# Cross-attention and feed-forward block on one core: later contexts in another place, first weight unit in halves, zeros multiplied, other orders

## The reference

```python
query = einsum('bnc,dc->bnd', ctx, Wq) + bq              # 128 wide
key   = einsum('bnc,dc->bnd', ctx, Wk) + bk
attention = softmax(einsum('bnd,bmd->bnm', query, key))  # 512 x 512 of each b
x = x + einsum('bln,bmn->blm', layernorm(x), attention)
n = layernorm(x)
# q(t): each block of 32 features scaled by its largest magnitude / 448,
#       rounded to fp8 e4m3, and scaled back to fp32
h = silu(q(n) @ q(gate_w).T) * (q(n) @ q(up_w).T)
out = x + q(h) @ q(down_w).T
```

## Time and profile before

| | |
|---|---|
| median of 3 runs | 617.62 us |
| the profiled execution: time | 618.75 us |
| its span | 617.0 us |
| PE busy, matmuls | 599.0 us, 97% |
| DVE busy | 495.3 us, 80% |
| ACT busy | 301.9 us, 49% |
| POOL busy | 42.4 us, 7% |
| chain that ended last, by engine | PE 89%, ACT 6%, SP's queue 2%, DMA 2% |

### The profile page before, as it was taken

The page is one execution under the profiler, slowest core; times in us unless marked ns, Lnnn a source line. Parts: engine busy times, 40 slices in busy tenths (PEclk is TensorE's granted clock), DMA queues, the critical chain, the costliest instruction groups (busy, mean ns, idle before and its releaser), DMA issues.

```text
span 617.0 us, 7089 instructions
## 1 busy us (share of the span) xinstructions
PE 599.0 (97%) x2624; PEld 276.9 (45%) x2624; DVE 495.3 (80%) x467; ACT 301.9 (49%) x449; POOL 42.4 (7%) x58
## 2 busy tenths in 40 slices
PE   4899989999999999999999999999999999999997
PEld 1535455444444444444444444444444444444443
DVE  5899999998999998996999999520149999999810
ACT  1899995645554545465455564502114232643420
POOL 1000000201000000101001110000000000010100
PEclk9999999999999999999999999999999999999999
DMA  8927769798987885968847758605000002777771
GB/s 336 410 76 168 223 191 261 176 266 211 204 223 199 209 211 141 217 120 170 205 95 155 158 110 185 119 1 85 1 1 1 2 0 37 134 122 134 122 135 34
DMA packets 147586, 90.18 MB, mean 146 GB/s; under 512 B 134240, under 2 KB 134368, under 8 KB 142816
## 3 DMA queue, kind: packets, MB, share of 16 engines
q1 hardware_dynamic: 142368, 63.78, 43.2%
q0 software_dynamic: 5184, 25.95, 18.7%
HBM read 25.76 MB, written 8.39 MB: 55 GB/s over the span
## 4 chain that ended last, share of the span: by engine, by line
PE 89%; ACT 6%; SPq 2%; DMA 2%; issue 1%; DVEq 0%; DVE 0%; ACTq 0%
PE bank L693 53%; PE bank L705 18%; PE bank L708 9%; PE bank L677 4%; PE bank L654 2%; ACT h L915 1%; PE bank L668 1%; ACT h L906 1%; PE bank L661 1%; DMA gu_hi<-in_ctxT 1%; SPq L377 1%; DMA xT<-hT 1%; ACT mag L870 1%; ACT hT L961 0%; ACT dn L927 0%
## 5 line engine op out<-in xcount | busy, mean ns | idle before, releaser
L693 PE MATMUL bank<-gu_hi,xT 128*128 128x512 f16 x1024 | 243.2, 379 | 0.4 <-DMA xT<-hT 0.4
L693 PEld LDWEIGHTS bank<-gu_hi,xT 128*128 128x128 f16 x1024 | 100.0, 98 | 121.8 <-DMA xT<-hT 1.1
L693 PE MATMUL bank<-gu_lo,xT 128*128 128x512 f16 x512 | 131.4, 379 | 0.0
L705 PE MATMUL bank<-dn,hT 128*128 128x512 f16 x512 | 113.1, 379 | 0.0
L1503 DVE SCALAR_TENSOR_TENSOR h<-bank,unscale,silu 128x512 f32<-128x512 f32 x64 | 46.5, 747 | 64.3 <-PE bank L693 60.4
L1000 ACT ACTIVATE silu<-bank,unscale 128x512 f32<-128x512 f32 x64 | 42.8, 682 | 102.8 <-PE bank L693 65.6
L705 PEld LDWEIGHTS bank<-dn,hT 128*128 128x128 f16 x512 | 50.1, 98 | 60.4
L693 PEld LDWEIGHTS bank<-gu_lo,xT 128*128 128x128 f16 x512 | 50.1, 98 | 60.4
L708 PE MATMUL bank<-dn,hT 128*128 128x512 f16 x256 | 57.9, 379 | 0.0
L677 PE MATMUL bank<-dn,h 128*128 128x512 f32 x128 | 55.7, 593 | 0.8 <-ACT dn L942 0.8
L1043 ACT ACTIVATE y<-bank,xnmr,odown 128x128 f32<-128x128 f32 x60 | 22.5, 456 | 52.6 <-PE bank L708 52.6
(11 more groups left out here) (99 smaller groups left out, 534.8 us busy)
## 6 DMA issues: line engine op xcount, KB each, us to landing
W<-in_units SPq DMA_DIRECT2D x12, 1024.0 KB, 5.7
W<-hT POOLq DMA_DIRECT2D x12, 1024.0 KB, 5.9
h<-W POOLq DMA_DIRECT2D x6, 1024.0 KB, 6.2
h<-in_xcols SPq DMA_DIRECT2D x4, 1024.0 KB, 10.6
out_y<-y POOLq DMA_DIRECT2D x15, 256.0 KB, 4.9
gu_hi<-in_ctxT SPq DMA_DIRECT2D x4, 512.0 KB, 10.2
h<-in_xrows SPq DMA_DIRECT2D x2, 1024.0 KB, 15.1
out_y<-h SPq DMA_DIRECT2D x2, 1024.0 KB, 7.6
```

Of the source, the lines that this page charges most:

```text
L693: last = pe.matmul(bank[:, :], xT[:, b % 2, part, k, :], w[:, c, g, j * 512:(j + 1) * 512], start=(j == 0 and not low), stop=(j == HT - 1 ...
L705: pe.matmul(bank[:, :], hT[:, r % 2, 0, k, :], dn[:, w, k, :], start=(k == 0 and w == 0), stop=False)
```

## The change

- Contexts 2 and 3 get a place of their own, early_xw, where the centered rows stand later, and are loaded at the start; every context has its own semaphore. center(0) waits for all eight projections.
- Unit 0 is loaded and reduced in two halves (load_half, load_rest, reduce_half, reduce_rest).
- DVE clears `zeros` first, and PE multiplies them 18 times ahead of the first projection (keep_zeros), and five times the identity ahead of the first energies (keep).
- New orders of products, roundings, banks and of all five lists. Among them: on SP load_columns(3), store_rows(1) and load_unit(4) come to stand behind the wait for the accumulation of unit 1; on ACT silu_of(3, 0) comes ahead of the exponentials of context 3; on PE products (3, 0) and (1, 0) come ahead of turn_probs(3, 0), and downs 3 to 6 and products (15, 2), (15, 3) change places with others; turn_rows_hi(3) and rows_rest(3) come later.

The instructions of all other steps are the same. The diff, cut; the rest of it is of the same kind, lines of the five lists in another order:

```diff
-        ctx = [ctx_all[:, n * 1024:(n + 1) * 1024].rearrange("p (t n) -> p t n", n=512) for n in range(2)]
...
+        ctx = [place[:, n * 1024:(n + 1) * 1024].rearrange("p (t n) -> p t n", n=512)
+               for place in (ctx_all, early_xw) for n in range(2)]
...
-        ctx_in = [sem(f"ctx_in{k}") for k in range(2)]
+        ctx_in = [sem(f"ctx_in{b}") for b in range(B)]
...
+            def load_half(u):
+                sp.dma_start(W[u][:, 0:UNIT // 2], units[u][:, 0:UNIT // 2]).then_inc(half_in, 16)
+
+            def load_rest(u):
+                sp.dma_start(W[u][:, UNIT // 2:], units[u][:, UNIT // 2:]).then_inc(w_in[u], 16)
+
...
-                if b >= 2:
-                    sp.wait_ge(proj_ready, 2 * (b - 1))
-                sp.dma_start(ctx[b % 2], ctx_cols[b]).then_inc(ctx_in[b % 2], 16)
+                sp.dma_start(ctx[b], ctx_cols[b]).then_inc(ctx_in[b], 16)
...
                 sp.dma_start_transpose(hT[:, r % 2, 1, :, :], hparts[:, 1, :]).then_inc(hT_in[1], 16)
-            load_unit(0)
+            load_half(0)
+            load_rest(0)
+            load_ctx(0)
             load_consts()
-            load_ctx(0)
             load_unit(1)
             load_unit(2)
+            load_ctx(3)
             load_ctx(1)
             load_columns(0)
             load_columns(1)
+            load_ctx(2)
             load_rows(0)
             load_rows(1)
             load_rows(2)
             load_rows(3)
-            load_ctx(2)
-            load_ctx(3)
             sp.wait_ge(*unit_rest_in(0))
             turn_unit_hi(0)
+            load_columns(2)
+            store_rows(0)
             turn_unit_lo(0)
             load_unit(3)
+            sp.wait_ge(*unit_rest_in(1))
             turn_unit_hi(1)
-            store_rows(0)
-            load_columns(2)
             load_columns(3)
+            turn_rows_hi(0)
+            turn_unit_hi(2)
+            turn_unit_lo(1)
+            turn_rows_lo(0)
             store_rows(1)
             load_unit(4)
-            sp.wait_ge(*unit_rest_in(1))
-            turn_unit_lo(1)
-            turn_unit_hi(2)
-            turn_rows_hi(0)
-            turn_rows_lo(0)
+            sp.wait_ge(*unit_rest_in(2))
             store_rows(2)
-            sp.wait_ge(*unit_rest_in(2))
+            load_unit(5)
+            turn_unit_lo(2)
...
             turn_hidden_lo(4)
-            sp.wait_ge(*rows_rest_in(3))
-            turn_rows_hi(3)
-            turn_rows_lo(3)
-            load_last()
-            turn_hidden_hi(5)
             sp.wait_ge(*hidden_rest_in(5))
             turn_hidden_lo(5)
+            turn_hidden_hi(5)
             turn_hidden_hi(6)
             turn_hidden_lo(6)
             turn_hidden_hi(7)
             turn_hidden_lo(7)
             turn_hidden_hi(8)
             turn_hidden_lo(8)
+            turn_rows_hi(3)
+            sp.wait_ge(*rows_rest_in(3))
+            load_last()
+            turn_rows_lo(3)
+            turn_hidden_lo(9)
             turn_hidden_hi(9)
...
             unit_rest(7)
-            unit_max(9)
             pool.wait_ge(wT_in[1], 128)
             unit_rest(8)
             unit_max(10)
-            pool.wait_ge(wT_in[1], 144)
+            pool.wait_ge(wT_in[0], 160)
             unit_rest(9)
             unit_max(11)
-            pool.wait_ge(wT_in[0], 176)
             unit_rest(10)
             pool.wait_ge(wT_in[0], 192)
...
+            pool.wait_ge(nT_in[0], 64)
+            rows_rest(3)
...
+            keep_zeros(18)
             pe.wait_ge(consts_in, 32)
             project(0, 0)
             project(0, 1)
+            keep("e0.0", 5)
...
             project(1, 0)
             project(1, 1)
             turn_probs(0, 0)
+            energies(1, 0)
+            project(2, 0)
             turn_probs(0, 1)
             turn_probs(0, 2)
+            project(2, 1)
             turn_probs(0, 3)
-            energies(1, 0)
+            project(3, 0)
+            project(3, 1)
             energies(1, 1)
             energies(1, 2)
             energies(1, 3)
-            project(2, 0)
-            project(2, 1)
-            project(3, 0)
-            energies(2, 0)
-            project(3, 1)
-            energies(2, 1)
-            energies(2, 2)
-            energies(2, 3)
             attend(0, 0)
             attend(0, 1)
...
+            product(3, 0)
+            product(1, 0)
             turn_probs(3, 0)
             turn_probs(3, 1)
             turn_probs(3, 2)
             attend(3, 2)
...
             product(11, 0)
             product(11, 1)
             product(11, 2)
+            product(9, 2)
+            down(3)
+            product(10, 0)
+            down(4)
+            down(5)
+            down(6)
+            product(9, 3)
+            product(10, 1)
             product(11, 3)
-            down(4)
+            product(10, 2)
+            product(10, 3)
             product(13, 0)
-            product(13, 1)
-            product(13, 2)
...
             down(7)
             down(8)
             down(9)
+            product(15, 2)
+            product(15, 3)
...
             take_projection(0, 0)
+            unit_magnitude(0)
             take_projection(0, 1)
-            unit_rescale(0)
-            unit_magnitude(0)
             exponential(0, 0)
             exponential(0, 1)
             exponential(0, 2)
             exponential(0, 3)
             take_projection(1, 0)
+            weigh(0, 0)
+            unit_rescale(0)
             take_projection(1, 1)
-            weigh(0, 0)
+            take_probs(0, 0)
             weigh(0, 1)
             weigh(0, 2)
             weigh(0, 3)
-            take_probs(0, 0)
+            unit_rescale(1)
             row_means(0)
             row_variances(0)
-            unit_rescale(1)
+            take_probs(0, 1)
             exponential(1, 0)
-            exponential(1, 1)
             unit_rescale(2)
...
+            unit_hi(2)
+            unit_lo(1)
+            row_means(3)
+            row_variances(3)
+            unit_magnitude(3)
+            attended_variances(1)
+            silu_of(3, 0)
+            unit_rescale(3)
             exponential(3, 0)
             exponential(3, 1)
-            unit_magnitude(3)
-            unit_lo(1)
-            rows_hi(0)
-            unit_hi(2)
             exponential(3, 2)
             exponential(3, 3)
+            silu_of(1, 0)
             weigh(3, 0)
             weigh(3, 1)
...
-                if b == 1:
+                if b == 0:
+                    dve.wait_ge(proj_ready, 2 * B)
+                elif b == 1:
...
+            def reduce_half(u):
+                dve.wait_ge(half_in, 16)
+                own.done(dve.tensor_reduce(scale[:, u, 0:NB // 2], blocks(W[u][:, 0:UNIT // 2]), AX.X, ALU.max,
+                                           apply_absolute_value=True))
+
+            def reduce_rest(u):
+                dve.wait_ge(w_in[u], 16)
+                reduced[u] = own.done(dve.tensor_reduce(scale[:, u, NB // 2:], blocks(W[u][:, UNIT // 2:]), AX.X, ALU.max,
                                                         apply_absolute_value=True))
...
+            dve.memset(zeros, 0.0).then_inc(zeros_ready, 1)
+            reduce_half(0)
+            reduce_rest(0)
             unit_largest(0)
             unit_scale(0)
-            unit_power(0)
             unit_reduce(1)
+            unit_reduce(2)
             row_max(0, 0)
             row_max(0, 1)
             row_max(0, 2)
             row_max(0, 3)
-            unit_reduce(2)
+            unit_power(0)
+            unit_largest(1)
             row_sum(0)
-            unit_largest(1)
+            unit_largest(2)
+            unit_power(1)
...
-            center(1)
-            rows_scale(1)
+            unit_reduce(4)
+            row_sum(3)
+            unit_largest(4)
+            hidden_of(3, 0)
+            unit_round(3)
+            hidden_of(1, 0)
+            unit_dequant(3)
+            rows_round(1)
+            unit_power(4)
             hidden_of(0, 0)
-            attended_means(2)
-            unit_largest(4)
-            unit_scale(4)
-            rows_round(1)

```

652 lines of the change are left out of this document (315 added, 337 removed), and 10 rows, old and new, of the table products.

## The result

The changed kernel takes 621.88 us (median of 6 runs, 621.06 to 623.67); the kernel before, beside it, 618.26 (617.29 to 618.98). The ratio is 1.0063, with an interval of 1.0045 to 1.008: it is slower by 0.6%, where 614.6 and faster was forecast. The profiled execution, the longest of the six, took 623.67 with a span of 621.9, against 618.75 and 617.0 before; the profiled difference is 4.9 us, that of the medians 3.6, so a sum over the two traces is some 1.3 too large for the medians.

What follows compares the result with a forecast made beforehand. PE, 97% busy, bounds it, with VectorE just in time; PE's loss falls from 19.0 to 14.1 us, but VectorE's order lets only 3.0 through: 614.6 against the median 617.62, range 611.6 to 620.5.

Steps and rivals of the forecast that it cites:

- The front: Start of the kernel: warm clock, halved unit 0, early contexts; energies at 13.65, attend(0) at 34.9 instead of 43.6.
- PE's gap ahead of turn_probs(3): Silu ahead of the last exponentials needs three table loads, so PE loses 2.7 us (bounds 0 to 5.4).
- DVE's sum: VectorE's work up to rows 2: hidden_dequant(0) ends at 252.0, product (8, 0) starts at 299.3, 3.0 us gained.
- the walk: Following all five engines' new lists, each step at its duration in the trace of before; profiled span 614.0 us.
- signs that the forecast named as proving it wrong: A PE gap ahead of product (2, 1), (2, 2) or (13, 0) would make the prediction wrong.
- The bank lists ask nothing more: In the front, banks add no further waits; nearest is energies(1, 1) at 32.3 behind take_probs(0, 1) at 32.0.
- B: Rival: VectorE falls behind at the last exponentials and is 6.8 us later, giving 620.5; chance 0.20.
- A: Rival: PE decides and VectorE keeps up, so all of the 4.9 us is kept, 612.7; chance 0.22.
- C: Rival: the zeros do not warm the clock, energies start 3 us later, 616.5; chance 0.08.
- D: Rival: nothing kept, a just-in-time place (rows 3, unit 3) takes back the 3 us, 617.6; chance 0.10.
- The late risks: Near the end, downs 4 to 6, rows 3 at product (13, 0), last products: counted 0, bounds 0 to 3.5 us lost.

Runs made afterwards that it cites:

- exp_first: Changed kernel with the exponentials of context 3 again ahead of attended_variances(1) and silu_of(3, 0) on ScalarE; 620.15 us, ratio 1.0036 to the kernel before.
- loads_short: Changed kernel with loads of units 6 to 11 cut to 1/16 of their bytes (output not the reference's); 617.25 us, ratio 0.9994 to the kernel before.
- lo3_first: Changed kernel with turn_unit_lo(3) ahead of turn_rows_hi(1) in SP's queue; 622.29 us, ratio 1.0083 to the kernel before.
- bank_early: Changed kernel with hidden_of(1, 2) and (1, 3) moved ahead of unit_round(11) on VectorE; 621.64 us, ratio 1.006 to the kernel before.
- best1: Changed kernel with reductions 6 and 7 later, context 3's exponentials ahead of the silu, hidden_of(1, 2), (1, 3) ahead of unit_round(11); 620.70 us, ratio 1.0045.

## Why the prediction was wrong

*The front was right.* Energies at 14.11 (forecast 13.65), attend(0) at 35.63 (34.9), end of attend(2) at 90.94 (90.8). Three table loads, at 94.48, 96.81 and 100.91:

```profile
94.48 1.28 ACT L1006 ACT_TABLE_LOAD   x1
...
96.81 1.28 ACT L933 ACT_TABLE_LOAD   x1
...
100.91 1.28 ACT L1006 ACT_TABLE_LOAD   x1
102.21 0.69 ACT L1006 ACTIVATE silu<-bank,unscale 128x512 f32<-128x512 f32 x1
```

Each costs 1.30 to the start of the next activation, and PE's gap ahead of turn_probs(3) is 1.86 where 2.7 was forecast. By the figure of the Trainium skill (ScalarE: Activation LUTs, Table sets: the hidden batching unit), about 2.7 a switch, the forecast of that wait would have been 5.4, an estimate; both traces show 1.30, and the measurement decides. VectorE idles 2.86 + 1.00 = 3.9 there, where 3.7 was forecast, but for another reason in the main, so that the closeness is partly luck: 2.86 are for the load of unit 4, which the forecast took as there in time, and only 1.00 for the exponentials. Without the load wait the exponentials would have held VectorE until the same 100.93 (101.5 forecast); without the exponentials (exp_first) it goes on at 99.40. It ends unit_dequant(4) at 133.5 (134.1).

*The step that failed is in DVE's sum, the stretch behind that*, "units 5 to 11 by scale 2.9, round 4.6, dequant 2.3, reduce 2.3, largest and power 0.7, each behind its load". I summed the work and took each load as there. From unit_dequant(4) to the end of hidden_dequant(0) I had 252.0 - 134.1 = 117.9; it took 256.7 - 133.5 = 123.2. Before, it was 253.0 - 130.3 = 122.7; with the 3.8 of work that the new list has already done by then, and 1.0 less of waits, this made my 117.9. Measured, the waits for loads are 10.3 instead of 1.5, those for PE and the silu 0.5 instead of 4.2, those for a magnitude 0.3 less: 4.8 more in all instead of 1.0 less, which is 5.8 and gives 123.7 against 123.2. The wait had to be read from the loads' side: unit u + 3 can't come before unit u is dequantised, made high, accumulated, made low and loaded, 20.1 us from 133.5 to 153.67 for unit 7. With the waits taken away (loads_short) hidden_dequant(0) ends at 250.6 and product (8, 0) starts at 299.9, where the walk had 252.0 and 299.3. So with the loads out of the way the walk's two times come out within 1.4. What the loads' bytes and the faster transposes behind them each do in that run is open, as said above.

*A smaller miss of the same kind* is turn_unit_lo(3), forecast to land at 131 where PE wants it at 132.5; PE waited until 133.75. SP's turns of rows 1 and of unit 3's low part took 3.53 and 3.56 to issue, where the walk had 1.9 each. The gap of 1.66 that this makes is one of the signs that the forecast named as proving it wrong; lo3_first took it away and gained nothing. One row of before is also misread there: of the two transposes at 270.07, turn_hidden_hi(0) is the first, not the second (that one goes out at 283.6). It was issued at 270.07 and down 4.4 to 4.9 later, one to two microseconds ahead of down(0), so the slack stated was right.

*"The bank lists ask nothing more" was checked for the front alone.* Product (7, 0) has its bank from product (1, 2), whose hidden_of stands behind hidden_dequant(0). By my own times VectorE would have emptied it at 252.7 at the earliest, and PE asked for it at about 250.8 (271.5 less four products of 5.18): a gap of 1.9 that the sum lacks. It would hardly have changed the forecast, since PE would then have waited less for hidden row 0 and rows 2, for which the sum has 0.9 and 1.1. With VectorE 4.7 later it is 5.27. But bank_early shows that the missing entry is not the cause: without it the wait only has another name.

*The clock's second price was not in any case.* I costed each wait at its length. A wait of 5.27 cost 1.7 more in the trace of after; in best1 one of 2.01 did.

*The rivals.* B, that VectorE falls behind and decides, happened. Its own rule, 617.6 plus what rows_dequant(2) ends behind 288.6, gives 617.6 + 2.8 = 620.4 with the measured 291.4 (289.10 + 2.29); 621.88 was measured. Its cause was half right: the late exponentials are 1.7, and transposes issued behind loads are slow (5.47, 5.60 and 5.30 for turn_unit_lo(4), (6) and (8)), but the larger share, 4.6, is that of the load waits, in which these transposes have an unmeasured part. The chance of 0.20 was too low, since forecast and A both needed VectorE to keep a pace that nothing in the trace of before had tested with loads asked for earlier. C (the zeros don't warm) and D did not happen. The range ended at 620.5 and the time lies 1.4 above it.

*The late risks* (rows 3 at product (13, 0), the downs 4 to 6, the last two products) were rightly set at 0: PE has no gap behind 308.77.

*A smaller point.* Loads_short reproduces my walk in the trace but takes 617.25, not 614.6. 1.4 is between its span (615.4) and mine (614.0). The other 1.2 is the base: I took the 3.0 us from the median, but worked them out against a profiled execution of 618.75, 0.3 to 1.1 over the medians of the kernel before.

## What to carry to other kernels

Where an engine works in order over a few rotating places, a walk of its list needs the time at which each load can come, worked round the whole cycle of its place, and not only the engine's work; a reduction placed earlier in the list buys nothing if its load cannot be earlier. A gain in the front of such a kernel is worth what the just-in-time engine keeps of it, and a bank or place behind that engine must be followed to the end of the list. Extra work that keeps TensorE's clock up pays only if what comes next is loaded in time: in one kernel here it lost 0.6%, in the other it was worth 0.6%.

## What was not expected of the hardware

- A wait of PE of 4.13 us brought the granted clock to 0.50 in the next 4 us and 0.77 in the 4 behind; one of 5.27 brought 0.68 and 0.89, and one of 2.01 (best1) brought 0.57. Waits of 1.66, 1.86 and 2.30 left it at 1.00, and 17 small matmul pairs in place of the one of 4.13 kept it there.
- A transpose that SP issues directly behind a 1 MB load takes 5.07 to 5.60 us to issue (four times between 148 and 254 us in the kernel after); the three of them that stand behind a load of 64 KB in the run loads_short take 1.82 to 2.02.
- Of two 1 MB accumulations issued 1.8 us apart (134.00 and 135.77) the second took 8.23 and the first 6.1; the median of the twelve of units is 6.0. The longest of the twelve, 9.9 at 91.48, had no other accumulation beside it.
